# Scores of a lattice attention stage: a 128-row product with zero padding, or two 64-row products issued as a pair

## The reference, cut to what matters

```
scores = einsum('bhqd,bhkd->bhqk', q, k) / 8          # q, k: 1024 x 64
int_scores = (abs(scores) * 1618).astype(int32)
penalty = where(int_scores % 3 == 0, 1/PHI, 1)        # mod 9 in {0, 3, 6}
attn = softmax(scores * penalty)
attn = attn * (sin(C1*attn) * exp(-attn*attn/PHI) + cos(C2*attn))
ctx = einsum('bhqk,bhkd->bhqd', attn, v)
```

## Time and profile before

| what | value |
|---|---|
| device time, 3 runs | median 6219.48 us (6199.0 to 6223.66) |
| the profiled execution | 6179.57 us, span 6177.8 us |
| busy over the span | PE 83%, DVE 68%, ACT 63%, POOL 57%; weight loads (PEld) 49% |
| mean granted clock of PE | 0.938 of full speed |
| lattice stage | about 162 to 4698 us of the span |
| chain of waits that ended last | covers the end of the program only (PE 7% of the span in the experts) |

### The profile page before, as it was taken

How to read it: one execution, slowest core, us unless ns; L and a number is a source line. 1 busy time by engine, 2 the same in 40 slices (tenths; PEclk the granted TensorE clock), 3 DMA queues, 4 the chain that set the end, 5 groups by cost and what they waited for, 6 DMA issues and landing times. The chain is left out here.

```text
span 6177.8 us, 99317 instructions
## 1 busy us (share of the span) xinstructions
PE 5130.0 (83%) x28905; PEld 3048.5 (49%) x28905; DVE 4184.2 (68%) x7201; ACT 3919.1 (63%) x5322; POOL 3537.1 (57%) x3151
## 2 busy tenths in 40 slices
PE   2688888888888888888888888888886999997999
PEld 1344444444444444444444444444444777775777
DVE  2577777777777777777777777777774545555443
ACT  1577777777778777787777877778773222222222
POOL 4677777777777777777777777777772101000111
PEclk9899999999999999999999999999997989898999
DMA  0000000000000000000000000000000000000000
GB/s 11 15 8 11 7 7 7 7 11 7 7 7 9 9 7 7 7 9 9 7 7 7 9 9 7 7 7 9 9 6 8 1 1 1 1 1 16 5 4 6
DMA packets 34157, 45.63 MB, mean 7 GB/s; under 512 B 24473, under 2 KB 24537, under 8 KB 34010
## 3 DMA queue, kind: packets, MB, share of 16 engines
q1 hardware_dynamic: 31962, 43.49, 2.5%
q0 software_dynamic: 2048, 0.14, 0.1%
HBM read 39.40 MB, written 4.19 MB: 7 GB/s over the span
## 5 line engine op out<-in xcount | busy, mean ns | idle before, releaser
L588 PE MATMUL banks<-ident,att 128*128 128x128 f32 x8192 | 1148.7, 287 | 405.4 <-DVE ag L520 244.1
L588 PEld LDWEIGHTS banks<-ident,att 128*128 128x128 f32 x8192 | 945.8, 147 | 999.0 <-DVE ag L520 614.0
L630 PE MATMUL banks<-kT,qT 128*128 128x512 f32 x2048 | 1144.0, 658 | 274.6 <-DVE mx L549 265.1
L390 POOL TENSOR_TENSOR sinb<-sinb,ag 128x1024 f32<-128x1024 f32 x512 | 1281.2, 2505 | 83.7 <-ACT sinb L461 68.4
L540 DVE SCALAR_TENSOR_TENSOR mag<-near,mag 128x512 f32<-128x512 int32 x1024 | 865.7, 850 | 483.2 <-POOL near L406 474.5
L647 PE MATMUL outp<-work,vo 128*64 128x512 f32 x2048 | 1045.0, 635 | 0.0
L647 PE MATMUL outp<-sinb,vo 128*64 128x512 f32 x2048 | 1044.9, 635 | 0.0
L400 POOL TENSOR_SCALAR mag<-mag 128x512 f32<-128x512 f32 x1024 | 689.3, 677 | 565.8 <-DVE mag L540 531.1
L406 POOL TENSOR_SCALAR near<-mag 128x512 int32<-128x512 f32 x1024 | 796.4, 778 | 355.8 <-ACT mag L479 293.8
L479 ACT ACTIVATE mag<-banks 128x512 f32<-128x512 f32 x1024 | 599.2, 592 | 279.8 <-PE banks L630 279.4
L497 DVE TENSOR_TENSOR work<-banks,work 128x1024 f32<-128x1024 f32 x512 | 625.3, 1221 | 188.5 <-ACT work L455 185.5
(11 more groups left out here) (199 smaller groups left out, 7085.9 us busy)
## 6 DMA issues: line engine op xcount, KB each, us to landing
x<-xT_dram SPq DMA_DIRECT2D x128, 256.0 KB, 3.4
xT_dram<-xT SPq DMA_DIRECT2D x8, 256.0 KB, 2.9
out<-hres SPq DMA_DIRECT2D x8, 256.0 KB, 2.6
base<-in_L_tok_turns,idx POOLq DMA_INDIRECT x64, 2.2
wqk<-in_L_attn_Wq SPq DMA_DIRECT2D x64, 16.0 KB
wqk<-in_L_attn_Wk SPq DMA_DIRECT2D x64, 16.0 KB
wqk<-in_L_attn_bq SPq DMA_DIRECT2D x64, 0.2 KB
wqk<-in_L_attn_bk SPq DMA_DIRECT2D x64, 0.2 KB
```

The lines of the kernel that those rows point to most:

```text
L390: nc.gpsimd.tensor_tensor(sinb[:, k % RING], sinb[:, k % RING], ag[:, k], ALU.mult).then_inc(tmul, 1)
L588: mm = nc.tensor.matmul(turn_pair(k)[:, c, i * P:(i + 1) * P], att[:, p, 4 * half + i, kt * P:(kt + 1) * P], ident[:], is_transpose=True, ...
L630: nc.tensor.matmul(score_bank(n), qT[:, p, (n // 2) * P:(n // 2 + 1) * P], kT[:, p, (n % 2) * 512:(n % 2 + 1) * 512], start=True, stop=Tru ...
```

## The change

`wqk` holds the 64 columns of Wq twice and then those of Wk (192 columns, six loads instead of four). The projection is now three steps: two with the doubled q (512 tokens each; both partition halves of `outp` receive the same q), and one in which two matmuls of 64 columns put the keys of tokens 0 to 511 in partitions 0 to 63 and those of 512 to 1023 in partitions 64 to 127. ACT makes three copies of 128 partitions instead of four of 64. A score tile contracts over 64 rows: tile n (even) over rows 0 to 63 and tile n+1 over rows 64 to 127, issued one right after the other, and only when the filter of tile n-2 is done. The zero fill goes. The lists of steps are new, with `STEPS` 88 instead of 44.

```
-        wqk = sb("wqk", [D + 1, P])
+        wqk = sb("wqk", [D + 1, P + D])
-        kT = sb("kT", [P, 2, S])
+        kT = sb("kT", [P, 2, S // 2])
-        STEPS = 44
-        SCORE = [0, 1, 6, 8, 10, 13, 15, 18, 19, 21, 26, 28, 29, 33, 35, 38]
+        STEPS = 88
+        SCORE = [1, 2, 15, 19, 21, 27, 31, 38, 39, 50, 51, 55, 62, 66, 71, 74]
...
-            pool.wait_ge(consts, 5)
-            nc.gpsimd.memset(qT[:], 0.0).then_inc(consts, 1)
-            pool.wait_ge(consts, 6)
-            nc.gpsimd.memset(kT[:], 0.0).then_inc(consts, 1)
...
-                cols = slice(c * 512, (c + 1) * 512)
-                rows = slice(p * D, (p + 1) * D)
-                nc.scalar.activation(qT[rows, p, cols], outp[0:D], ACT.Copy, scale=QSCALE).then_inc(qk_sb, 1)
-                nc.scalar.activation(kT[rows, p, cols], outp[D:P], ACT.Copy).then_inc(qk_sb, 1)
+                if c == 2:
+                    nc.scalar.activation(kT[:, p], outp[:], ACT.Copy).then_inc(qk_sb, 1)
+                else:
+                    nc.scalar.activation(qT[:, p, c * 512:(c + 1) * 512], outp[:], ACT.Copy,
+                                         scale=QSCALE).then_inc(qk_sb, 1)
...
+                if c == 2:
+                    for half in range(2):
+                        mm = nc.tensor.matmul(outp[half * D:(half + 1) * D], wqk[:, P:P + D],
+                                              x[:, half * 512:(half + 1) * 512], start=True, stop=True)
...
-                        if a in SCORE:
+                        if a in SCORE and SCORE.index(a) % 2 == 0:
                             n = SCORE.index(a)
...
-                            wait(pe, filtered, NTILE * g + (n - 2 if n >= 3 else (0, -2, -1)[n]))
-                            nc.tensor.matmul(score_bank(n), qT[:, p, (n // 2) * P:(n // 2 + 1) * P],
-                                             kT[:, p, (n % 2) * 512:(n % 2 + 1) * 512],
-                                             start=True, stop=True).then_inc(qk, 1)
+                            wait(pe, filtered, NTILE * g + (n - 1 if n else 0))
+                            for c in range(2):
+                                rows = slice(c * D, (c + 1) * D)
+                                nc.tensor.matmul(score_bank(n + c), qT[rows, p, (n // 2) * P:(n // 2 + 1) * P],
+                                                 kT[rows, p], start=True, stop=True).then_inc(qk, 1)
```

More of the change, by code:

```diff
@@ L282, in lattice @@
         HALF = TB // 2
-        STEPS = 44
-        SCORE = [0, 1, 6, 8, 10, 13, 15, 18, 19, 21, 26, 28, 29, 33, 35, 38]
[L285 to L289, removed]
+        STEPS = 88
+        SCORE = [1, 2, 15, 19, 21, 27, 31, 38, 39, 50, 51, 55, 62, 66, 71, 74]
+        ABS, RND, KEEP, FACT, FILT, BIAS = 2, 2, 6, 6, 8, 12
+        EXP = [STEPS + o for o in [7, 12, 13, 14, 23, 28, 31, 32]]
+        GAUSS = [STEPS + o for o in [20, 22, 31, 32, 36, 37, 45, 46]]
+        SQ, GEXP, AG = 2, 2, 4
+        SINE = [STEPS + o for o in [56, 61, 64, 70, 71, 77, 78, 87]]
+        AV = [STEPS + o for o in [70, 76, 77, 84, 100, 101, 102, 113]]
         OUT = (AV[HALF - 1] + 1, AV[-1] + 1)
[L291 to L294, removed]
+        FOLD, ADD = OUT[1] + 1, OUT[1] + 3
+        PROJ, VAL, EV = (35, 37, 49), 60 + STEPS, 3
+        COS, MUL, RED, SIN, P3 = 2, 2, 6, 7, 7
+        NORM, TURNS = 2, 11
         DVE_ROWS = (TB // 2 - 1, TB - 1)
@@ L338, in load_q @@
                 if isinstance(t, int):
-                    wait(sp, projd, 2 * t)
+                    wait(sp, projd, 3 * t)
                 else:
@@ L343, in load_q @@
                 sp.dma_start(x[0:D, :], tokens(t)).then_inc(loadq, 16)
[L344 to L347, removed]
+                for c, (w, b) in enumerate(((Wq, bq), (Wq, bq), (Wk, bk))):
+                    cols = slice(c * D, (c + 1) * D)
+                    sp.dma_start(wqk[0:D, cols], w[:, bass.ds(h * D, D)]).then_inc(loadq, 16)
+                    sp.dma_start(wqk[D:D + 1, cols],
+                                 b.rearrange("(a n) -> a n", a=1)[:, bass.ds(h * D, D)]).then_inc(loadq, 16)
             def load_v(t):
@@ L353, in load_v @@
                 else:
-                    wait(sp, projd, 2 * (t + 3))
+                    wait(sp, projd, 3 * (t + 3))
                 sp.dma_start(x[0:D, :], tokens(t)).then_inc(loadv, 16)
@@ L464, in iteration @@
                     for g, p, a in stages(t, par, s):
-                        if a - 1 in GAUSS:
-                            d = GAUSS.index(a - 1)
+                        if a - SQ in GAUSS:
+                            d = GAUSS.index(a - SQ)
                             wait(act, xpose, NX * g + d + 1)
@@ L515, in iteration @@
                     for g, p, a in stages(t, par, s):
[L516 to L517 removed]
+                        if a - AG in GAUSS:
+                            d = GAUSS.index(a - AG)
                             wait(dve, gauss, TB * g + d + 1)
@@ L563, in _ @@
         def _(pe):
-            pe.wait_ge(consts, 7)
+            pe.wait_ge(consts, 5)
             def project(g, p, c):
-                wait(pe, loadq, 80 * (g + 1))
+                wait(pe, loadq, 112 * (g + 1))
                 if c == 0:
@@ L573, in project @@
                 else:
-                    wait(pe, qk_sb, 4 * g + 2)
-                nc.tensor.matmul(outp[:], wqk[:], x[:, c * 512:(c + 1) * 512], start=True, stop=True).then_inc(projd, 1)
-            project(0, 0, 0)
-            project(0, 0, 1)
+                    wait(pe, qk_sb, 3 * g + c)
+                if c == 2:
+                    for half in range(2):
+                        mm = nc.tensor.matmul(outp[half * D:(half + 1) * D], wqk[:, P:P + D],
+                                              x[:, half * 512:(half + 1) * 512], start=True, stop=True)
+                else:
+                    mm = nc.tensor.matmul(outp[:], wqk[:, 0:P], x[:, c * 512:(c + 1) * 512], start=True, stop=True)
+                mm.then_inc(projd, 1)
+            for c in range(3):
+                project(0, 0, c)
             def fill(g, p, k):
@@ L661, in iteration @@
                             last = isinstance(g, int) and g + 2 >= NHEADS
-                            wait(pe, qk_sb, 4 * NHEADS if last else 4 * (g + 3))
+                            wait(pe, qk_sb, 3 * NHEADS if last else 3 * (g + 3))
                             wait(pe, evac, 2 * g)
@@ L668, in iteration @@
                             mm.then_inc(vald, 1)
-                    for c in range(2):
+                    for c in range(3):
                         if s == PROJ[c] and (not isinstance(t, int) or t + 1 < NHEADS):
```

20 lines of the change are left out of this document (9 added, 11 removed).

## The result

The changed kernel takes 6758.36 us (median, 6735.77 to 6762.55) where the kernel before takes 6211.18 on the same chip: a ratio of 1.087 (95% interval 1.084 to 1.091). It is 547 us slower, 64 heads times 8.5 us. The profiled execution took 6735.77 us.

What follows compares the result with a forecast made beforehand. No engine was full; PE was taken to bound A, POOL B, ACT C. Per head -2.0 - 2.4 + 1.7 = -2.7 us, times 64 = -173; 6179.6 - 173 + 3 = 6010, plus 15: 6025 us, range 5870 to 6245.

Steps and rivals of the forecast that it cites:

- A: First stretch of a head, sines of blocks 0 to 3, PE fullest; forecast -2.0 us a head from less PE work.
- B: Middle stretch of a head, before the Gauss blocks, POOL fullest; -2.4 us from removed POOL roundings and an earlier DVE division.
- C: Last stretch of a head, the Gauss blocks, ACT fullest; forecast +1.7 us a head, from added ACT work and pair waits.
- a pair streams together: Score products on PE: both tiles of a pair overlap, 0.95 us a pair, bounds 0.86 and 1.72.
- DVE's division of block 3 ends ahead of POOL's third: Sign before the Gauss blocks: DVE's division comes first, so the first Gauss block starts sooner, -0.8 us a head.
- The value product's loads stay hidden: After the last projection: tokens land 3.4 us after issue, covered by ACT's Gauss work with about 1 us to spare.
- at 2.4 GHz (1.00): PE's granted clock in the Gauss stretch, read from the profile before; the forecast gave no us for a change in it.
- a lone half is not cheaper: Score products on PE: one over 64 rows keeps the 0.43 to 0.48 us spacing of 128; only overlap pays.
- alone moves nothing: Two AV steps put ahead of PE's 2.96 us filter wait: no gain by itself, since POOL bounds that stretch.
- The fourth rival: Pairs make scores and transpositions wait for filters at seven places: +2.1 us a head, 6315 us; chance 0.15.
- Its test: PE's wait for `mx` before the scores: near 4 us a head if forecast holds, 8 or more if coupling is real.
- the limit that I had named: In A, the block chain makes ACT and DVE the next limit, so about half of PE's 3.7 us comes through.

Runs made afterwards that it cites:

- e3: The kernel before put in the order of the new lists, with its single tiles over 128 rows and two projections; 6391 us, 1.029.
- e1: The kernel before with its order and single tiles, only the score matmul contracting over 64 rows instead of 128; 6535 us, 1.052.
- e16: The kernel before with single tiles, q and k in rows 0 to 63 and the score product over 65 rows; 6297 us, 1.013.
- e10: The kernel before with two AV steps moved ahead of PE's long wait and DVE's division of block 3 ahead of its TURNS; 6319 us, 1.022.
- e4: The changed kernel with every score tile issued alone at its own step, over its 64 rows, with its own wait; 6642 us, 1.068.
- e6: The kernel before in the new lists, its padded 128-row products issued in pairs with the pair's wait; 7003 us, 1.132.
- e19: The kernel before with the filter multiplying the factor by itself in SBUF, score left out, waits as they were; 6584 us, 1.059.
- e17: The changed kernel with the filter multiplying the factor by itself in SBUF, score left out, pair's wait as it was; 7069 us, 1.138.

## Why the prediction was wrong

The forecast was 6025 us and 0.74 for faster. By its own steps, a head, with the means of the table (A 17.3 to 18.9, B 24.7 to 24.3, C 28.0 to 35.3):

| step | forecast | measured |
|---|---|---|
| a pair streams together | 0.95 us for 1.72 | 1.06 from its start to the next (median), two tiles of before 1.88: right |
| A | -2.0 | +1.6 |
| B | -2.4 | -0.4; the lists alone (e3) -1.6 |
| C | +1.7 | +7.3; the lists alone (e3) +3.9, 64 rows alone (e1) +4.6 |
| sum | -2.7 | +8.5 |

**Right.** The overlap: from the transposition record ahead to PE's next record behind, at full clock and without a wait, a pair takes 1.27 us and two tiles of before 1.99 (medians), a saving of 0.7 where 0.8 was forecast. The Trainium skill, "TensorE: Matmul & The Clock Gate", Part 3, says that tiles in different row groups run side by side, and the trace agrees (four records of a pair in 1.13 us, two of a single tile in e1 in 1.12). DVE's division of block 3 ends ahead of POOL's third, as this piece of DVE's and POOL's rows after shows:

```profile
2044.88 3.17 POOL L393 TENSOR_SCALAR att<-att,rs 128x1024 f32<-128x1024 f32 x2 [0.27 <-DVE rs L513]
...
2045.69 0.85 DVE L524 TENSOR_SCALAR att<-att,rs 128x1024 f32<-128x1024 f32 x1
```

L524 ends at 2046.5, the second of the two L393 at 2048.1. The value product's loads stay hidden: its copy waited 5.9 us in the whole program. POOL lost its work in B, as counted, and ACT gained its work in C, as counted (27.7 us busy against 26.1, +1.6 where +1.5 was forecast); but C is 34.9 us long and ACT no longer bounds it.

**Wrong: the sum had no term for the clock.** The step "at 2.4 GHz (1.00)" in C was read as a property of the stretch. It held for 128-row products in the old lists: C's clock is 0.97 before, 0.75 with 64 rows (e1), 0.90 with the new lists (e3) and 0.76 after. e1 alone shows it: 4.6 of its 5.2 us a head lie in C, 5.2% for an edit that I costed at nothing ("a lone half is not cheaper"). A lone half is dearer, by 0.29 us between transpositions and by the clock that falls with it. Of the 5.2%, 1.3 are there at 65 rows, without a change of mode, and the rest comes with the split (e16). My row for a 64-row product was one at full clock and alone, 1.02 us long where a half tile of e1 takes 1.12. It had neither the change of mode nor what such products do to the clock around them. With the rule cited at e1 (the Trainium skill, "TensorE: Matmul & The Clock Gate", Part 1), a lower clock for a kernel that works PE less was a candidate; I gave it no rival.

**Wrong: the order.** In B I wrote that AV5 and AV6 ahead of the wait "alone moves nothing". With the division moved too, it costs 2.4 us a head (e10): PE then idles in front of the first transposition, and C runs at a lower clock. C was forecast from ACT's list alone.

**Wrong in size: the pair's wait.** In C it was 0.2, with bounds 0 and 3 in all; 6.3 us of waiting stand there in front of pairs. The fourth rival had the mechanism, its place and the reason: three banks, of which a pair takes two, and transpositions in order behind it. Its test was 8 us of `mx` wait a head; the measured 6.1 lies between its marks. Its price, 6315, was too small, because it had neither the clock nor the order. It is not the main loss: set against the overlap's gain, pairs cost 1.2 us a head (after to e4). What the pairing alone costs, without the overlap, is 10.1% (e6 to e3).

**Wrong: A and B.** A was to gain from PE. PE's rows in A did get shorter (13.8 us busy of 18.0: 16.4 of 17.8), and A did not. In front of its subtraction of the turns PE waits for DVE's product `work` 421 us over the program, 91 before, and 358 with the lists alone (e3). So the block chain over ACT and DVE, the limit that I had named, is likely its bound; I still took half. B's gain exists with the lists alone, and goes into POOL's idle time once 64 rows and pairs are added.

In order, the loss is 2.9% for the lists (e3), 3.8% for 64 rows with the third projection (e4 to e3), 1.8% for the pairs (after to e4, their overlap gain set against their waits). The order of taking them matters: pairs in padded form cost 10.1%. What stays open is which chain carries the rest of the pairs' cost beside the bank, how the split's own time and the low clock share the cost of 64 rows, and which of e10's two moves makes C longer. None of these kernels beats the one before.

## What to carry to other kernels

PE time that is freed where another engine sets the end buys nothing, and the operands and the order that free it can cost the granted clock: look at the clock of a stretch as something that the edit can change, and give it a term. Two products issued together need two free banks at the same moment, so before pairing count the banks and find what frees each. Try changed operands, changed order and pairing one at a time; here each was a loss by itself that the gain of the overlap did not cover.

## What the runs showed that I had not expected

The rows that a product uses change the clock that PE is granted, in the same order and with alike waits: 64 rows 1.052, 65 rows 1.013, 96 rows 1.001 of the time before. The shortest record is 589 to 592 ns in all of them. The large step is the one row from 65 to 64, where the array is split.

A filter on DVE with both operands in SBUF is slower than with one in PSUM while POOL works beside it. Its instances in e19, half of them in each form (shortest, median and longest ns):

```profile
L549 DVE CUSTOM_DVE_ANT_0 att<-mag x512: 671/1095/2740, 182.0 to 5034.4; 128x512 f32<-128x512 f32 x171
L549 DVE CUSTOM_DVE_ANT_0 att<-mag,mx x512: 732/746/2598, 183.1 to 5041.6; 128x512 f32<-128x512 f32 x171
```

On average the two take 1295 and 974 ns; with the bank as second operand they take 681 and 740 in the kernel before. In e17 the first form takes 692 ns (median) where POOL is idle beside it and 1064 where POOL is busy for over half of it. POOL's L400 takes 677 ns before and 810 in e19, and that program is 5.9% slower.
